# Macaron layer on one core: the second expert list opened with complete sequences 4 and 5, and the last four attention chains moved forward in the slot table

## Chip, core and metric

One NeuronCore of a Trainium2 chip runs the whole kernel. The metric is device time in microseconds (us), the median of several executions. The engines are TensorE (PE, its weight loads PEld), VectorE (DVE), ScalarE (ACT), GpSimd (POOL) and SyncE (SP). Each works through its own instructions in order and waits on semaphores.

## What is computed

Eight sequences of 512 tokens with 128 features (4096 tokens, 32 blocks of 128) go through a sandwich: half an expert layer, a state-space attention layer, half an expert layer.

```
x = x + 0.5 * ffn(layernorm(x))      # 12 experts, top 3 per token
x = x + attn(layernorm(x))           # gates, a scan over time, layernorm, gated projections
x = x + 0.5 * ffn(layernorm(x))      # the same experts again

ffn:  logits = x @ Wg; topw, sel = top_k(logits, 3); w = softmax(topw)
      h = gelu(x @ Wup[e] + bup[e]);  y = h @ Wdown[e] + bdown[e];  out = sum_k w_k y_sel_k
```

## The kernel before

**Tiles and lists.** The expert work is cut into 225 tiles of 128 rows that belong to one expert. For a tile PE does four matmuls up (L1017), ACT four gelus (L1205) and a copy of the expert's weights (L1088), PE four matmuls down (L1032), and DVE adds the bias into `Ys` (L2059). The tiles stand in four lists: list 0 (tiles 0 to 59, first expert layer, sequences 0 to 3), list 1 (tiles 60 to 106, first layer, sequences 4 to 7, with what was left of 0 to 3), list 2 (tiles 107 to 153, second layer, sequences 0 to 2) and list 3 (tiles 154 to 224, second layer, sequences 3 to 7). Within a list the "front" tiles are those that can be filled from the list's first few sequences; `FRONT` (L43) says how many sequences, `GA` (L44) how many groups of four tiles that gives: 3 groups, 12 tiles, for list 1.

**Routing of the rows.** POOL moves rows by indirect DMAs of 128 rows, one for each block of tokens and each of its three choices, so 12 a sequence. A scatter (`scatter_x`, L806) writes a sequence's normalised rows into the list's table `xs`; SP then loads a tile's rows from there (`load_rows`, L646 to L661). Before a list's first load SP waits until the scatters of its `FRONT` sequences have landed. A gather (`gather_y`, L809 to L824) brings a token's three expert rows back from `ys` to `YG`; before the first one of a list it waits until all tiles of the list are stored. In list 3 the expert rows are scattered one transfer a tile (`yk`, L832), with the 36 gathers of list 2 between them. POOL's order is fixed by the table `POOL` (L155): "Y" are the gathers of a sequence after the first expert layer, "K" its scatters for the second.

**Attention chains.** Between the two expert layers each sequence goes through a chain of some 23 steps, which the table `CHAIN` (L130) puts into tile slots of list 1 and 2: the numbers count tiles from tile 60, one column for each sequence. G0 and G2 on DVE add the gathered expert rows to X (L1330), S1 is the norm on DVE (L1279 to L1303), G on ACT writes the normalised rows (L1111), A1 on PE transposes them (L878), A2 to A7 are the projections, T to L choose the experts for the second layer (N on DVE and ACT, L1120), and K counts places so that POOL can scatter (K on PE is L937). Each engine does the steps of a slot after its work on the slot's tile. So a step that is not ready blocks the tiles behind it.

**First lists' tables.** How the tiles of list 0 and list 1 are shared out among experts is worked out on DVE in step Q4 (L1884), at tile 12 of list 0. Tables for list 2 are made by DVE in the steps A0 to A2 at tiles 98 to 100 and Z0 to Y3 at tiles 104 to 111, for list 3 in the same way from tile 147 and tile 159.

**Start of a list.** PE transposes the first four tiles of a new list one by one (`turn_first`, L998): the first of them stands in the last tile of the list before, behind that tile's up matmuls and ahead of the down matmuls of the tile two before it.

Of the kernel before, what the change touches and what calls it, by code (L numbers as in the profile page):

```python
# [10 lines left out]
ALU = mybir.AluOpType  # L11
# [3 lines left out]
P = 128  # L15
# [15 lines left out]
AT = tuple(4 * s[0] for s in SEQS)  # L31
# [337 lines left out]
def macaron_kernel(nc, a, out):  # L369
    with ExitStack() as ctx:  # L370
        def sb(name, shape, dt=F32):
            return ctx.enter_context(nc.sbuf_tensor(name, shape, dt))

        def sem(name):
# [228 lines left out]
        def _(e):  # L603
# [151 lines left out]
        def _(e):  # L755
# [513 lines left out]
        def _(e):  # L1269
# [541 lines left out]
            def second(kind, s):  # L1811
# [57 lines left out]
                elif kind == "Q3":  # L1869
# [14 lines left out]
                elif kind == "Q4":  # L1884
# [31 lines left out]
                    dv.on(e.tensor_tensor(step2[:], basB[:, 0:E], basC[:, 0:E], ALU.subtract))  # L1916
                    e.wait_ge(s_dv, dv.n - 2)
                    dv.on(e.scalar_tensor_tensor(don4[:], rem[:], 0.0, remW[:], ALU.max, ALU.min))
                    e.wait_ge(s_dv, dv.n)
                    dv.on(e.tensor_tensor(don4[:], don4[:], donC[:], ALU.add))  # L1920
                    e.wait_ge(s_dv, dv.n)
# [227 lines left out]
```

## Time and profile before

| | |
|---|---|
| median of 3 runs | 615.02 us (612.63 to 616.59) |
| the profiled execution's own time | 614.01 us |
| its span, first to last instruction | 612.3 us |
| mean granted TensorE clock | 0.973 |
| busy, share of the span | PE 91%, ACT 84%, POOL 66%, DVE 60% |

Busy PE is partly modelled, because matmuls overlap. The times of the rows are us from the start of the span. A share of the span is a mean over stages with different limits, so the stages are read one by one.

### The profile page before, as it was taken

The page shows a single profiled execution, that of the slowest core. Times are in us where ns is not written, and L with a number is a line of the kernel's source. Part 1 is how long each engine was busy: PE and PEld are TensorE (multiplying, and loading weights), DVE is VectorE, ACT ScalarE, POOL GpSimd, SP SyncE. Part 2 cuts the span into 40 slices and gives each one's busy share as a digit, 9 for nine tenths or more (in the row PEclk, how much of TensorE's full clock was granted, in tenths as well). Part 3 has the DMA queues.
Part 4 walks back from the last instruction along what each step waited for, and adds up shares of the span by engine and source line. Part 5 has one row for each costly group of instructions (what it writes and reads, how often), then busy time and mean ns, then how long its engine had stood idle before and what let it go on. Part 6 is the DMA issues. An engine that isn't in the chain of part 4 may idle for free.

```text
span 612.3 us, 17470 instructions
## 1 busy us (share of the span) xinstructions
PE 559.2 (91%) x4625; PEld 523.3 (85%) x4625; DVE 369.6 (60%) x1735; ACT 514.3 (84%) x1462; POOL 403.8 (66%) x424
## 2 busy tenths in 40 slices
PE   6899887999999999989899798998799799999996
PEld 6789887999999888868799697877699799999992
DVE  7977899441111586988775578997727632232225
ACT  4547994799989989889988699988689789989885
POOL 1076577777746777137677777767777777777771
PEclk9789999899999999999999799999999999999999
DMA  7997243243463434112355333232254532433264
GB/s 197 316 234 212 54 135 88 79 131 104 123 180 101 123 87 118 52 48 71 91 160 136 87 88 98 83 107 67 67 148 111 139 89 72 117 90 85 64 232 138
DMA packets 99127, 72.28 MB, mean 118 GB/s; under 512 B 13520, under 2 KB 91910, under 8 KB 99033
## 3 DMA queue, kind: packets, MB, share of 16 engines
q1 hardware_dynamic: 83032, 43.62, 25.7%
q0 software_dynamic: 13024, 26.11, 15.0%
q10 hardware_dynamic: 2976, 1.44, 0.8%
q8 instruction: 42, 0.69, 0.5%
q14 instruction: 53, 0.43, 0.2%
HBM read 37.08 MB, written 34.75 MB: 117 GB/s over the span
## 4 chain that ended last, share of the span: by engine, by line
PE 32%; DVE 21%; POOL 17%; issue 12%; ACT 8%; DMA 7%; ACTq 1%; DVEq 1%; POOLq 0%; SPq 0%
PE ps L1017 12%; PE ps L1032 12%; POOL YG L822 10%; DMA YG<-ys,SY 4%; POOL xs L806 4%; ACT hT L1205 3%; POOL yk L832 3%; DVE YG L1717 2%; DMA yk<-Ys,row 2%; PE ps L1007 2%; DVE st L1274 2%; DVE Ys L2059 1%; DVE X L1330 1%; PE ps L987 1%; DVE X L1316 1%
## 5 line engine op out<-in xcount | busy, mean ns | idle before, releaser
L1205 ACT ACTIVATE hT<-ps,BU 128x128 f32<-128x128 f32 x900 | 261.5, 392 | 43.9 <-PE ps L1017 34.5
L1017 PE MATMUL ps<-xT,WT 128*128 128x128 f32 x1800 | 243.1, 279 | 8.6 <-ACT hT L1205 5.5
L1032 PE MATMUL ps<-WD,hT 128*128 x1800 | 240.9, 277 | 6.8 <-DVE Ys L2059 6.8
L1017 PEld LDWEIGHTS ps<-xT,WT 128*128 128x128 f32 x1800 | 222.9, 194 | 18.2 <-issue 16.4
L1032 PEld LDWEIGHTS ps<-WD,hT 128*128 128x128 f32 x1800 | 221.4, 194 | 8.4 <-issue 8.3
L806 POOL DMA_INDIRECT xs<-XN,SX x144 | 142.4, 989 | 70.7 <-issue 63.3
L822 POOL DMA_INDIRECT YG<-ys,SY x132 | 130.6, 990 | 49.3 <-issue 35.4
L1088 ACT ACTIVATE WT<-WU 128x512 f32 x225 | 150.2, 668 | 7.5 <-DVE eW L1750 3.3
L2059 DVE TENSOR_TENSOR Ys<-ps,BD 128x128 f32<-128x128 f32 x225 | 54.8, 285 | 146.5 <-PE ps L1032 140.4
L832 POOL DMA_INDIRECT yk<-Ys,row x71 | 70.7, 995 | 21.9 <-issue 12.2
L793 POOL DMA_INDIRECT xl<-xna,SG x24 | 23.1, 961 | 37.4 <-DMA xna<-XN 27.6
L1330 DVE SCALAR_TENSOR_TENSOR X<-YG,WK,X 128x128 f32<-128x128 f32 x96 | 26.6, 345 | 13.8 <-DMA YG<-ys,SY 13.2
L1178 ACT ACTIVATE xT<-ps 128x512 f32<-128x512 f32 (+1 forms) x52 | 32.6, 627 | 1.6 <-PE ps L987 0.8
L987 PE MATMUL ps<-ident,xl 128*128 128x128 f32 x205 | 31.3, 275 | 0.0
L1120 ACT ACTIVATE XN<-X,na,nr 128x128 f32<-128x128 f32 x64 | 26.4, 510 | 4.4 <-DVE na L1303 4.4
L793 POOL DMA_INDIRECT xl<-xnc,SG x24 | 23.0, 957 | 7.3 <-issue 5.8
L1316 DVE SCALAR_TENSOR_TENSOR X<-YG,WK,X 128x128 f32<-128x128 f32 x36 | 12.7, 354 | 20.8 <-DMA YG<-ys,SY 19.8
L987 PEld LDWEIGHTS ps<-ident,xl 128*128 128x128 f32 x205 | 24.6, 144 | 0.0
L1007 PE MATMUL ps<-ident 128*128 128x128 f32 x130 | 22.8, 353 | 1.6 <-POOL ident L759 1.6
L1007 PEld LDWEIGHTS ps<-ident 128*128 128x128 f32 x130 | 21.4, 190 | 1.7 <-POOL ident L759 1.6
L1274 DVE BATCH_NORM_STATS2 st<-X 128x6 f32<-128x128 f32 x96 | 21.0, 277 | 0.7 <-DVE SL L1641 0.4
L904 PEld LDWEIGHTS ps<-wgc,sT 128*128 128x128 f32 x128 | 16.0, 197 | 4.5 <-ACT sT L1104 4.0
(366 smaller groups left out, 592.2 us busy)
## 6 DMA issues: line engine op xcount, KB each, us to landing
ys<-Ys SPq DMA_DIRECT2D x41, 256.0 KB
xl<-xs SPq DMA_DIRECT2D x94, 64.0 KB
xl<-xs SPq DMA_DIRECT2D x71, 66.0 KB
WU<-in_L_ffn_Wup_dram SPq DMA_DIRECT2D x12, 256.0 KB, 4.6
WD<-in_L_ffn_Wdown_dram SPq DMA_DIRECT2D x12, 256.0 KB, 4.7
YG<-yk SPq DMA_DIRECT2D x4, 768.0 KB, 6.2
xs<-XN,SX POOLq DMA_INDIRECT x144
YG<-ys,SY POOLq DMA_INDIRECT x132
```

The costliest lines, as they stand in the source:

```text
L793: e.indirect_dma_start(xl[m % NXL][:, k % 4, 0:D], None, xna if k < NA[0] else xnb if k < NM else xnc, bass.IndirectOffsetOnAxis(SG[:, k:k ...
L806: e.indirect_dma_start(xs[n], bass.IndirectOffsetOnAxis(SX[n][:, k, t:t + 1], 0), XN[:, AT[n] + t, 0:DX[n]], None).then_inc(s_air[j % AIR] ...
L822: e.indirect_dma_start(YG[:, (AT[n] + t) % 16, k, :], None, ys[n], bass.IndirectOffsetOnAxis(SY[n][:, t // 4, k, t % 4:t % 4 + 1], 0)).the ...
L832: e.indirect_dma_start(yk, bass.IndirectOffsetOnAxis(row[g % NROW][:, k % 4:k % 4 + 1], 0), Ys[(GROUP0[n] + g) % NYS][:, k % 4, :], None, ...
L987: i = e.transpose(ps[:, j * P:(j + 1) * P], xl[m % NXL][:, j, 0:D], ident[:])
L1007: e.transpose(HB[0][:, 0:P], ident[:], ident[:])
L1017: x = e.matmul(HB[i % 2][:, c * P:(c + 1) * P], WT[i % NW][:, c, :], xT[m % 2][:, j * P:(j + 1) * P], start=True, stop=True)
L1032: x = e.matmul(YB[u % 2][:, j * D:(j + 1) * D], hT[i % 3][:, c * P:(c + 1) * P], WDf[:, bass.ds(r + c * P, P)], start=(c == 0), stop=(c == ...
L1088: e.activation(WT[i % NW][:], WU[:, :, bass.ds(wu_at.pop((GROUP0[n] + k // 4, k % 4)), D)], ACT.Copy).then_inc(s_wt0, 1)
L1205: x = e.activation(hT[i % 3][:, c * P:(c + 1) * P], HB[i % 2][:, c * P:(c + 1) * P], ACT.Gelu, bias=BU[:, bass.ds(b + c, 1)])
L1274: dv.on(e.bn_stats(st6[:, t, :], src))
L2059: e.tensor_tensor(Ys[m % NYS][:, k % 4, :], YB[u % 2][:, j * D:(j + 1) * D], BD[:, bass.ds(bd_at.pop((m, k % 4)), D)], ALU.add).then_inc(s ...
```

## The change

Three things are changed, and the arithmetic of the layer stays the same.

1. `FRONT` of list 1 goes from 3 sequences to 2 and means something else there: the front is now 6 groups, 24 tiles, that hold every row of sequences 4 and 5 (and whatever of 6 and 7 fills those tiles). So their results are complete after tile 83. Step Q4 works this out with six more DVE instructions. SP's wait ahead of a list's first load is now for all the list's scatters, in list 1 and in list 3 too; only list 2 keeps the wait for its front (two sequences).
2. POOL's order gets the gathers of sequences 4 and 5 right behind those of sequence 3, ahead of the scatters of sequences 0 to 2. They wait for the stores of list 1's first 24 tiles alone.
3. In `CHAIN` every step of sequences 4 and 5 moves 8 tiles forward, of sequence 6 some 7, of sequence 7 some 5.

```
-FRONT = (HS, 3, 2, 3)
+FRONT = (HS, 2, 2, 3)

-    ("V", "G0", (8, 13, 19, 27, 54, 58, 65, 72)),
+    ("V", "G0", (8, 13, 19, 27, 46, 50, 58, 67)),
...
-    ("PV", "K", (33, 38, 44, 53, 75, 81, 86, 89)),
+    ("PV", "K", (33, 38, 44, 53, 67, 73, 79, 84)),

-POOL = (("Y", 0), ("Y", 1), ("Y", 2), ("Y", 3), ("K", 0), ("K", 1), ("K", 2), ("Y", 4), ("Y", 5), ("Y", 6), ("Y", 7),
+POOL = (("Y", 0), ("Y", 1), ("Y", 2), ("Y", 3), ("Y", 4), ("Y", 5), ("K", 0), ("K", 1), ("K", 2), ("Y", 6), ("Y", 7),
         ("K", 3), ("K", 4), ("K", 5), ("K", 6), ("K", 7))

                 if g == 0:
-                    for w in scattered(n, FRONT[n]):
+                    for w in scattered(n, FRONT[n] if n == 2 else len(SEQS[n])):
                         e.wait_ge(*w)

-                    for m in range(GROUP0[n + 1] - NYS, GROUP0[n + 1]):
+                if k == 0 and (t == 0 or n == 1 and t == 4 * FRONT[1]):
+                    done = GROUP0[1] + GA[1] if n == 1 and t == 0 else GROUP0[n + 1]
+                    for m in range(done - NYS, done):
```

On POOL, behind the last scatters for list 1, the kernel before has this order (xl are list 0's rows, xs the scatters, YG the gathers, yk the stores of list 3):

```order
L793 DMA xl<-xnc,SG 128x128
L806 DMA xs<-XN,SX 32384x128 x20
L822 DMA YG<-ys,SY 128x128 x48
L806 DMA xs<-XN,SX 32384x128 x36
L822 DMA YG<-ys,SY 128x128 x48
L806 DMA xs<-XN,SX 32384x132 x60
L832 DMA yk<-Ys,row 7680x128 x2
```

and the changed kernel this one:

```order
L794 DMA xl<-xnc,SG 128x128
L807 DMA xs<-XN,SX 32384x128 x20
L826 DMA YG<-ys,SY 128x128 x72
L807 DMA xs<-XN,SX 32384x128 x36
L826 DMA YG<-ys,SY 128x128 x24
L807 DMA xs<-XN,SX 32384x132 x60
L836 DMA yk<-Ys,row 7680x128 x2
```

So 24 gathers now stand ahead of the 36 scatters of sequences 0 to 2, of which the first 24 are those that list 2 waits for.

On DVE, at tiles 106 and 107, the last of list 1 and the first of list 2, the kernel before has A7 of sequence 3 (X<-X,ps) and then tables of list 2:

```order
L2059 TENSOR_TENSOR Ys<-ps,BD 128x128
L1437 TENSOR_TENSOR X<-X,ps 128x512
L1619 TENSOR_TENSOR tk<-tk,stp 1x420
L1622 TENSOR_SCALAR ei<-EF 128x35
L1624 TENSOR_REDUCE RF<-tk 1x35
L2059 ISA
L2059 TENSOR_TENSOR Ys<-ps,BD 128x128
L1629 SCALAR_TENSOR_TENSOR RR<-iotl,RF 1x35
```

and the changed kernel:

```order
L2075 TENSOR_TENSOR Ys<-ps,BD 128x128
L1441 TENSOR_TENSOR X<-X,ps 128x512
L1334 SCALAR_TENSOR_TENSOR X<-YG,WK,X 128x128 x6
L1278 BN_STATS st<-X 128x6 x2
L1623 TENSOR_TENSOR tk<-tk,stp 1x420
L1626 TENSOR_SCALAR ei<-EF 128x35
L1628 TENSOR_REDUCE RF<-tk 1x35
L2075 ISA
L2075 TENSOR_TENSOR Ys<-ps,BD 128x128
L1633 SCALAR_TENSOR_TENSOR RR<-iotl,RF 1x35
```

G0 of sequence 4 has come in between; G2 and S1 of sequence 4 come in the same way at tiles 108 and 109, ahead of the norm N' of sequence 3 at tile 110.

On ACT, behind the gelus of tile 110, the kernel before writes the rows of sequence 3 for the second expert layer (N, L1120):

```order
L1205 ACTIVATE hT<-ps,BU 128x128
L1088 ISA
L1088 ACTIVATE WT<-WU 128x512
L1120 ACTIVATE XN<-X,na,nr 128x128 x4
L1205 ISA
L1205 ACTIVATE hT<-ps,BU 128x128
```

and the changed kernel does so too (L1124), with G of sequence 4 (L1115) behind it:

```order
L1209 ACTIVATE hT<-ps,BU 128x128
L1092 ISA
L1092 ACTIVATE WT<-WU 128x512
L1124 ACTIVATE XN<-X,na,nr 128x128 x4
L1115 ACTIVATE XN<-X,na,nr 128x128 x4
L1209 ISA
L1209 ACTIVATE hT<-ps,BU 128x128
```

G of sequence 4 was behind tile 118 before.

## Rows read from the trace of the kernel before

**Rows 1.** Waits of PE, 195 to 450: total us, times, longest.

```profile
PE ps L878 <- ACT XN L1111: 8.1, 4, 4.7
PE ps L937 <- DVE MC L1377: 4.8, 4, 2.8
```

**Rows 2.** Timeline of PE: start, us, line, out<-in, [idle before <-releaser].

```profile
177.89 0.27 PE L998 MATMUL ps<-ident,xl 128*128 128x128 f32 x1
...
305.45 0.27 PE L998 MATMUL ps<-ident,xl 128*128 128x128 f32 x1
...
319.95 0.60 PE L987 MATMUL ps<-ident,xl 128*128 128x128 f32 x4
...
341.22 1.11 PE L878 MATMUL ps<-ident,XN 128*128 128x128 f32 x4 [4.68 <-ACT XN L1111]
...
442.33 0.20 PE L937 MATMUL ps<-M,LT 128*128 128x48 bf16 x1 [2.83 <-DVE MC L1377]
...
450.40 0.27 PE L998 MATMUL ps<-ident,xl 128*128 128x128 f32 x1
```

**Rows 3.** Busy time by engine (PE, PEld, DVE, ACT, POOL), clock, DMA; one stretch.

```profile
340.00:347.00 7.00, 5.78 (x22) 5.00 (x23) 2.94 (x12) 5.34 (x16) 5.17 (x7) 0.51 0.19 49
```

**Rows 4.** Timeline of SP's queue: start, us, line, loads of list 1, 2, 3.

```profile
171.30 4.36 SPq L661 DMA_DIRECT2D xl<-xs  x8
...
301.25 4.36 SPq L661 DMA_DIRECT2D xl<-xs  x8
...
445.86 4.33 SPq L661 DMA_DIRECT2D xl<-xs  x8
```

**Rows 5.** Timeline of POOL.

```profile
108.41 0.99 POOL L793 DMA_INDIRECT xl<-xnc,SG  x1 [0.30 <-issue]
...
175.86 0.97 POOL L806 DMA_INDIRECT xs<-XN,SX  x1 [0.30 <-issue]
...
268.96 0.99 POOL L806 DMA_INDIRECT xs<-XN,SX  x1 [21.03 <-issue]
...
298.73 0.96 POOL L806 DMA_INDIRECT xs<-XN,SX  x1 [0.30 <-issue]
...
460.53 0.99 POOL L832 DMA_INDIRECT yk<-Ys,row  x1 [0.30 <-issue]
```

**Rows 6.** POOL's groups, 460 to 600: busy, mean ns of one, idle before.

```profile
L832 POOL DMA_INDIRECT yk<-Ys,row x71 | 70.7, 995 | 21.9 <-issue 12.2 <-DMA yk<-Ys,row 4.9 <-DVE Ys L2059 3.6
```

**Rows 7.** Chain that ended last, at 184: start, us, a store's landing.

```profile
183.67 1.69 DMA ys<-Ys
```

**Rows 8.** Busy time by engine as in rows 3, three short stretches of DVE work.

```profile
77.80:80.60 2.80, 2.02 (x16) 1.86 (x16) 2.50 (x21) 2.80 (x9) 2.06 (x3) 1.00 0.17 51
...
335.12:337.22 2.10, 1.42 (x13) 1.18 (x12) 2.10 (x8) 0.09 (x1) 1.49 (x3) 1.00 0.41 112
337.25:339.49 2.24, 0.00 (x0) 0.00 (x0) 1.93 (x14) 0.00 (x0) 1.63 (x3) 1.00 0.15 38
```

**Rows 9.** POOL's groups, 180 to 250, as in rows 6.

```profile
L822 POOL DMA_INDIRECT YG<-ys,SY x48 | 47.4, 987 | 23.7 <-issue 14.3 <-DMA ys<-Ys 9.4
```

**Rows 10.** Timeline of DVE.

```profile
237.83 0.88 DVE L2059 TENSOR_TENSOR Ys<-ps,BD 128x128 f32<-128x128 f32 x4 [0.34 <-PE ps L1032]
...
308.56 0.69 DVE L1437 TENSOR_TENSOR X<-X,ps 128x512 f32<-128x512 f32 x1 [0.24 <-PE ps L977]
...
311.06 0.29 DVE L2059 TENSOR_TENSOR Ys<-ps,BD 128x128 f32<-128x128 f32 x1 [0.71 <-PE ps L1032]
...
312.88 0.29 DVE L2059 TENSOR_TENSOR Ys<-ps,BD 128x128 f32<-128x128 f32 x1 [1.03 <-PE ps L1032]
...
457.59 0.29 DVE L2059 TENSOR_TENSOR Ys<-ps,BD 128x128 f32<-128x128 f32 x1 [1.33 <-PE ps L1032]
```

**Rows 11.** Timeline of ACT.

```profile
319.86 1.65 ACT L1120 ACTIVATE XN<-X,na,nr 128x128 f32<-128x128 f32 x4 [0.96 <-DVE na L1303]
```

**Rows 12.** PE's up matmuls (L1017, eight passes a tile) in one stretch.

```profile
135.00:165.00 30.00, 16.90 (x128) 15.57 (x128) 1.00 0.41 116
```

More of the change, by code:

```diff
@@ L42 @@
 HS = 3
-FRONT = (HS, 3, 2, 3)
-GA = tuple(-((E * (P - 1) - (K * (AT[1] * (n == 1) + 4 * f) - FULL * (n == 1)) * P) // P) // 4 for n, f in enumerate(FRONT))
+FRONT = (HS, 2, 2, 3)
+GA = tuple((K * (AT[1] + 4 * f) + E - FULL) // 4 if n == 1 else -((E * (P - 1) - K * 4 * f * P) // P) // 4
+           for n, f in enumerate(FRONT))
 NA = tuple(4 * g for g in GA)
@@ L428, in macaron_kernel @@
             "wB", "remB", "endB", "basB", "don1", "don2", "donC", "remC", "endC", "basC", "endR", "basR"))
-        donW, remW, endW, basW, don4 = (sb(n, [P, EX]) for n in ("donW", "remW", "endW", "basW", "don4"))
+        donW, remW, endW, basW, don4, remX = (sb(n, [P, EX]) for n in ("donW", "remW", "endW", "basW", "don4", "remX"))
         nt6, remL, endL, basL, dltL, stpL, c6 = donC, remC, endC, basC, basB, step3, mixed
@@ L822, in gather_y @@
                 e.indirect_dma_start(
-                    YG[:, (AT[n] + t) % 16, k, :], None, ys[n],
+                    YG[:, (AT[n] + t) % 16, k, :], None, ys[n][0:(NTL[0] - NM + NA[1]) * P] if n == 1 and t < 4 * FRONT[1] else ys[n],
                     bass.IndirectOffsetOnAxis(SY[n][:, t // 4, k, t % 4:t % 4 + 1], 0)).then_inc(s_air[j % AIR], 16)
@@ L1877, in second @@
                     dv.on(e.tensor_tensor(cnt[:, 0:E], total, c4[:], ALU.add))
-                    dv.on(e.scalar_tensor_tensor(c7[:], part, -float(P - 1), c4[:], ALU.add, ALU.add))
+                    dv.on(e.tensor_tensor(c7[:], part, c4[:], ALU.add))
                     e.tensor_tensor(CT[:, a:], rows, by_token(c4, t), ALU.add).then_inc(s_sl0, 1)
@@ L1901, in second @@
                     dv.on(e.tensor_tensor(remW[:], donW[:], donC[:], ALU.subtract))
-                    e.wait_ge(s_dv, dv.n)
+                    dv.on(e.tensor_tensor(remX[:], nte[:], donW[:], ALU.subtract))
+                    e.wait_ge(s_dv, dv.n - 2)
                     dv.on(e.tensor_tensor_scan(endC[:], one[:], remC[:], float(NM), ALU.mult, ALU.add))
+                    e.wait_ge(s_dv, dv.n - 2)
                     dv.on(e.tensor_tensor_scan(endW[:], one[:], remW[:], 0.0, ALU.mult, ALU.add))
-                    e.wait_ge(s_dv, dv.n)
+                    e.wait_ge(s_dv, dv.n - 2)
+                    dv.on(e.tensor_tensor_scan(rem[:], one[:], remX[:], 0.0, ALU.mult, ALU.add))
+                    e.wait_ge(s_dv, dv.n - 1)
                     dv.on(e.tensor_scalar(endW[:], endW[:], endC[:, E:EX], None, ALU.add))
@@ L1909, in second @@
                     dv.on(e.tensor_scalar(lim3[:], donC[:, 0:E], float(P), None, ALU.mult))
-                    e.wait_ge(s_dv, dv.n - 2)
-                    dv.on(e.tensor_tensor(rem[:], endW[:], remW[:], ALU.subtract))
-                    dv.on(e.tensor_tensor(basW[:], endW[:], donW[:], ALU.subtract))
+                    e.wait_ge(s_dv, dv.n - 4)
+                    dv.on(e.tensor_tensor(rem[:], rem[:], remX[:], ALU.subtract))
+                    e.wait_ge(s_dv, dv.n)
+                    dv.on(e.tensor_scalar(rem[:], rem[:], endW[:, E:EX], None, ALU.add))
                     e.wait_ge(s_dv, dv.n)
                     dv.on(e.tensor_scalar(rem[:], rem[:], -1.0, float(NTL[0] + NA[1]), ALU.mult, ALU.add))
-                    dv.on(e.tensor_tensor(step3[:], basC[:, 0:E], basW[:, 0:E], ALU.subtract))
[L1916 to L1921, printed above, removed]
+                    e.wait_ge(s_dv, dv.n)
+                    dv.on(e.scalar_tensor_tensor(remX[:], rem[:], 0.0, remX[:], ALU.max, ALU.min))
+                    e.wait_ge(s_dv, dv.n)
+                    dv.on(e.tensor_tensor(remW[:], remW[:], remX[:], ALU.add))
+                    dv.on(e.tensor_tensor(don4[:], donW[:], remX[:], ALU.add))
+                    e.wait_ge(s_dv, dv.n - 1)
+                    dv.on(e.tensor_tensor_scan(endW[:], one[:], remW[:], 0.0, ALU.mult, ALU.add))
+                    e.wait_ge(s_dv, dv.n)
+                    dv.on(e.tensor_scalar(endW[:], endW[:], endC[:, E:EX], None, ALU.add))
+                    dv.on(e.tensor_tensor(step2[:], basB[:, 0:E], basC[:, 0:E], ALU.subtract))
+                    e.wait_ge(s_dv, dv.n - 1)
+                    dv.on(e.tensor_tensor(basW[:], endW[:], don4[:], ALU.subtract))
+                    e.wait_ge(s_dv, dv.n)
+                    dv.on(e.tensor_tensor(step3[:], basC[:, 0:E], basW[:, 0:E], ALU.subtract))
                     dv.on(e.tensor_tensor(rem[:], nte[:], don4[:], ALU.subtract))
```

42 rows, old and new, of the table CHAIN are left out of this document.

## Prediction, made before the changed kernel ran

> **What bounds the kernel now.** I read the clock and busy shares first: PE is busy for 91% of the span, so time is to be had only where PE waits, and I went on to PE's waits by releaser, then to PE's timeline around each wait, then back along POOL, SP and DVE. In lists 1 and 2 one group stands out: the transposes that open a chain (A1) wait for the rows that ACT writes in step G, 8.1 us in four waits, one of them 4.7 [rows 1]. That one ends at 341.22 [rows 2]: A1 of sequence 4 at tile 119. It waits because the gathers of sequence 4 stand on POOL behind the scatters of sequences 0 to 2. The wait also costs clock: the granted clock in the seven us from 340 is 0.51, so half rate [rows 3]. Seven us at 0.51 lose 3.4, less the half of the 1.2 us in which PE was idle anyway: 2.8. So what the change goes for is worth 4.7 + 2.8 = 7.5 us.
>
> The reader is to see three more places, where PE does not wait now but is close to it. A list begins with the transpose L998, at 177.89, 305.45 and 450.40 [rows 2], and SP issues the loads it needs at 171.30, 301.25 and 445.86 [rows 4]. For list 2 the load follows the last awaited scatter of POOL (sequence 1's, issued at 298.73 [rows 5]) by 2.5 us: that list starts as soon as POOL lets it, with little to spare. And from 460.53 [rows 5] POOL works without a break to the end: its 71 stores of list 3 have 0.31 us of idle time before them on average [rows 6], the same as transfers that wait for nothing.
>
> **The change part by part.** The sum is made against the profiled execution's 614.0 us, which lies 1.0 below the median of 615.0. "Later" is against the kernel before.
>
> Step 1, list 1's start. SP now waits for all 48 scatters of list 1. The last is issued at 175.86 [rows 5]; with the 2.5 us seen at list 2 the load goes out at 178.4 instead of 171.3. From load to transpose the trace shows 6.6, 4.2 and 4.5 us, none of which is the shortest possible. The nearest thing below is a store that landed 1.7 us after its issue [rows 7]. I take 2.2, near that row, since a landing and one semaphore hop are all that is in it; the bounds are 1.7 and 4.2. So L998 comes at 180.6, 2.7 later (2.2 to 4.7). Behind SP's wait stands the store of tiles 52 to 55, which POOL's first gather awaits; that gather also awaits the store of tile 59, which is later still, so it adds nothing. At lists 2 and 3 it is the same with the stores of tiles 100 to 103 and 147 to 150.
>
> Step 2, six more instructions in Q4. Its later part, 20 instructions and one of the step's neighbour, takes 2.8 us [rows 8], 0.14 each, so 0.8 us, ahead of the one-hot rows that PE waits for in list 0. POOL does not see it: its first transfer with the new indices, at 108.41, waits for nothing [rows 5]. PE comes 0.8 later to list 1 and there waits 0.8 less for step 1. It counts as nothing, and as 0.8 if step 1 were not there.
>
> Step 3, list 2's start. The 48 gathers of 180 to 250 take 47.4 us and, without the first wait, 14.3 between them [rows 9], 1.285 each; 24 more are 30.8. They go into a gap of 21.0 us in which POOL waits for the first scatter of sequence 0 [rows 5]; 0.3 of that is a normal step. So the scatters come 30.8 - 20.7 = 10.1 later than the rest of the kernel. That rest is itself 2.7 later, as the gathers start when list 0 is stored. The spare time at list 2 was 4.2 - 2.2 = 2.0 us. PE waits 10.1 - 2.0 = 8.1 us in tile 106 (7.6 to 10.1), and everything behind it in PE's order, the down matmuls of tiles 104 to 106 included, waits with it. Cover there is none: PE works in order.
>
> Here a rule of the skill bears on the price of a gather. The 48 gathers of rows 9 ran at a mean of 987 ns beside the same DVE steps (G0, G2, S1) as the 24 added ones will. The Trainium skill (SBUF — State Buffer, section "Who interferes with whom") says that GpSimd writes the descriptors of such DMAs through ports that DVE can hold for a whole instruction. By it a gather could take longer the busier DVE is; the trace at hand bears that out only weakly, as the mean shows, and the rival on it stands below.
>
> Step 4, clock. A wait of 4.7 us cost 2.8 us at half rate [rows 3]; one of 8.1 I price the same (0 to 3.4).
>
> Step 5, tiles 106 to 111. When PE goes on, DVE has G0, G2 and S1 of sequence 4 to do between A7 and N' of sequence 3: 2.1 + 2.1 + 2.2 us (G2 and S1 from [rows 8], G0 taken like G2). Of its idle time there, 0.7 and 1.0 us [rows 10] go. So N' ends 4.7 later, and ACT's N, which stood idle 0.96 us for it and then took 1.65 [rows 11], begins 4.7 later. Behind it now comes G of sequence 4, as long again. PE has A1 of sequence 4 behind the transposes of tile 111, which end at 319.95 + 0.60 = 320.5 [rows 2]; in the same frame G ends at 319.86 + 4.7 + 1.65 + 1.6 = 327.8. That is 7.3 us of waiting. Step 4 shortens it: PE itself comes 2.8 later, and DVE's chain, which begins 3.1 us after the restart (308.56 [rows 10] against 305.45), some 1.5, since a tile's down matmuls and A7 ahead of it run at half rate. I take 7.3 - 2.8 + 1.5 = 6.0 (0 to 7.3; nothing, if DVE did more of this ahead than its order shows). In the old order the same G had no neighbour.
>
> Step 6, clock again after that wait: 2.8 (0 to 2.8).
>
> Step 7, what goes. The gathers of sequence 4 begin where the gap of 21.0 us began, at 268.96 - 21.0 + 0.3 + 2.7 = 250.9, and are done 15.4 later; tiles 80 to 83, for whose store they wait, were ready at 238.7 [rows 10], or 241.4 now. G0 asks for them at about 319, so this wait is gone: -7.5 (the 4.7 are sure, the 2.8 of clock nearly so). Sequences 5 to 7 keep their spacing of 4, 8 and 9 tiles (4, 7 and 7 before); I leave the other waits of list 2 as they are, the one of 2.8 at K of sequence 7 [rows 1] included, since its steps T to K still share one slot.
>
> Step 8, list 3's start. SP now waits for the scatters of sequence 7 too. K of sequence 7 ran on PE at 442.33, and from there to L998 it was 8.1 us [rows 2]. Now K is five tiles further ahead, at 128 / 8 = 16 tiles in 30 us [rows 12], 1.88 each: PE needs 17.5 us. POOL's first scatter follows K by 2.9 at most (460.53 less twelve of 1.28 is 445.2); I take 2.2, then 11 x 1.28 to the last issue, 2.5 to the load, 2.2 to the transpose: 21.0. PE waits 3.5 (0 to 6).
>
> Step 9, POOL in list 3. The end is POOL's chain of 71 stores and 36 gathers. It began at 460.53, behind the scatters of sequence 7, though tile 154 had been ready at 457.59 + 0.29 [rows 10]. Those scatters are over before list 3 begins now: -2.6 (0 at the worst).
>
> The sum: 2.7 + 8.1 + 2.8 + 6.0 + 2.8 - 7.5 + 3.5 - 2.6 = 15.8, so 614.0 + 15.8 = 629.8, rounded 630. What is late next is the start of list 2, in place of A1 of sequence 4.
>
> **Rivals.** About 1% is what a measurement of this kernel tells from no change.
>
> A, near even: list 2 starts late, but the chain of sequence 4 comes through at tile 111. For it speaks that DVE stands idle during PE's wait of step 3; against it that A7, G0 and the rest follow, in DVE's order, a store that needs PE. Without steps 5 and 6: 629.8 - 8.8 = 621.0.
>
> B, faster: the 24 gathers fit into POOL's gap, so the scatters are not late and only the old wait goes. That needs 20.7 / 24 = 0.86 us a gather in place of 1.285, or a gap that is longer. Rows 9 speak against it, the gap of 21.0 us speaks for it. Without steps 3 to 6: 614.0 + 2.7 - 7.5 + 3.5 - 2.6 = 610.1, and 606.6 if step 8 is hidden too.
>
> C, slower still: transfers on POOL are drawn out where DVE is busier than now. If each of the 24 gathers and the 24 scatters behind them took 0.2 us more, list 2 would start 48 x 0.2 = 9.6 later: 639.4. The rule named under step 3 would do this. The mean of 987 ns speaks against it.
>
> **How the numbers follow.** The forecast has 0.60, A 0.22, B 0.10, C 0.08. The forecast's own range, its steps at their bounds, is about 614 to 640: below, steps 4, 5 and 8 shrink together; above, 10.1 and 4.7 at the list starts. The range of 611 to 639 takes in A and ends short of B and of C. B counts as faster (0.07) when step 8 hides, else as within 1%, like A: 0.24 for the same, so 0.69 for slower by over 1%.
>
> **What would show it.** Right: PE's transpose L998 at list 2's start has a wait of about 8 us, released by SP's loads, with POOL's gap before the scatters gone; A1 of sequence 4 waits some 6 us for ACT behind tile 111, with a clock near 0.5 after each; no wait of 4 us is left near tile 119; L998 of list 3 waits 2 to 5 us. Wrong: PE passes tile 106 without a wait (then B), or tile 111 (then A), or POOL's transfers there show a mean well over 1.0 us (then C).

## Result, and the profile after the change

The changed kernel takes 648.09 us (median of 4 runs, 645.83 to 649.98) against 613.83 us for the kernel before on the same chip (611.92 to 616.59): a ratio of 1.055, 95% interval 1.049 to 1.061. Slower was right; the size was not: the change costs 34 us, where the prediction had 15.8 and a range that ended at 639. The profiled execution took 649.49.

From the profile's page: the span, PE's busy time, and the granted clock in 40 slices.

```profile
span 647.8 us, 17478 instructions
PE 575.5 (89%) x4625; PEld 537.7 (83%) x4625; DVE 371.6 (57%) x1741; ACT 516.7 (80%) x1462; POOL 405.1 (63%) x424
PEclk8788997999999999999787999899799999999999
```

The waits of PE in lists 1 and 2 of the changed kernel (195 to 485 us; total, times, longest), to be held against [rows 1]:

```profile
PE ps L882 <- ACT XN L1115: 11.2, 4, 6.4
PE ps L1002 <- DMA xl<-xs: 8.2, 2, 5.1
PE ps L941 <- DVE MC L1381: 7.6, 3, 4.2
PE ps L882 <- DVE X L1441: 2.6, 1, 2.6
PE ps L978 <- DVE tg L1437: 1.8, 1, 1.8
```

The same waits in PE's timeline (start, us, line, out<-in, idle before and releaser), the start of list 1 (184.52) included:

```profile
184.52 0.30 PE L1002 MATMUL ps<-ident,xl 128*128 128x128 f32 x1 [2.29 <-DMA xl<-xs]
320.26 0.45 PE L1002 MATMUL ps<-ident,xl 128*128 128x128 f32 x1 [5.11 <-DMA xl<-xs]
345.12 1.12 PE L882 MATMUL ps<-ident,XN 128*128 128x128 f32 x4 [6.36 <-ACT XN L1115]
386.05 1.12 PE L882 MATMUL ps<-ident,X 128*128 128x128 f32 x4 [2.59 <-DVE X L1441]
405.38 0.39 PE L978 MATMUL ps<-BO,ones 3*128 3x512 bf16 x1 [1.78 <-DVE tg L1437]
419.02 0.20 PE L941 MATMUL ps<-M,LT 128*128 128x48 bf16 x1 [2.96 <-DVE MC L1381]
463.90 0.22 PE L941 MATMUL ps<-M,LT 128*128 128x48 bf16 x1 [4.19 <-DVE MC L1381]
484.53 0.44 PE L1002 MATMUL ps<-ident,xl 128*128 128x128 f32 x1 [3.11 <-DMA xl<-xs]
```

In the order of the rows: the starts of lists 1 and 2; A1 of sequence 4 at tile 111; T of sequence 4 at tile 125; A7 of sequence 5 at tile 130; K of sequence 5; K of sequence 7; the start of list 3. The first three and the last were forecast. The four between them were not: there the kernel before has one wait above 1.3 us, the one of 2.83 at K of sequence 7 [rows 2].

Busy time by engine (PE, PEld, DVE, ACT, POOL), granted clock, DMA share and GB/s in eight stretches of the changed kernel. The last is the whole of list 2, from its first transpose to that of list 3:

```profile
317.30:327.50 10.20, 7.07 (x29) 6.15 (x30) 2.62 (x9) 2.57 (x9) 7.76 (x9) 0.50 0.52 155
341.20:348.00 6.80, 2.88 (x14) 2.89 (x15) 6.02 (x34) 5.68 (x15) 5.28 (x6) 0.50 0.20 54
385.60:389.00 3.40, 2.95 (x14) 2.95 (x15) 3.04 (x18) 3.08 (x9) 0.00 (x0) 0.50 0.51 140
406.00:409.40 3.40, 3.40 (x18) 3.40 (x17) 3.14 (x13) 0.00 (x0) 2.49 (x4) 0.51 0.49 143
419.70:423.10 3.40, 3.40 (x18) 3.40 (x17) 2.16 (x14) 2.67 (x7) 0.16 (x1) 0.50 0.00 0
460.70:467.50 6.80, 3.60 (x19) 3.60 (x20) 5.31 (x34) 2.94 (x9) 1.71 (x3) 0.50 0.05 16
484.50:487.90 3.40, 3.19 (x14) 2.94 (x15) 0.29 (x1) 1.84 (x6) 0.00 (x0) 0.51 0.50 120
...
320.26:484.53 164.27, 138.53 (x999) 125.49 (x1000) 107.66 (x510) 121.75 (x335) 93.41 (x94) 0.89 0.28 82
```

and the whole of list 2 in the kernel before:

```profile
305.45:450.40 144.95, 130.01 (x1001) 117.64 (x1000) 109.23 (x513) 122.89 (x339) 107.79 (x111) 0.96 0.36 100
```

So list 2 grew by 19.3 us with the same work: PE is idle 25.7 us of it in place of 14.9, and busy 8.5 longer, at a mean clock of 0.89 in place of 0.96. The half clock that was forecast is there around the two long waits (317.3 and 341.2), and it is there with the shorter ones too (385.6, 406.0, 419.7, 460.7).

A ledger from the three list starts (177.89, 305.45, 450.40 before [rows 2]; 184.52, 320.26, 484.53 after) and the two spans:

| part | measured | forecast |
|---|---|---|
| until list 1 starts | +6.6 | +2.7 (step 1) |
| list 1, until list 2 starts | +8.2 | +8.1 (step 3) |
| list 2, until list 3 starts | +19.3 | +7.6 (steps 4 to 8) |
| list 3 and the end | +1.4 | -2.6 (step 9) |
| sum | +35.5 | +15.8 |

Of the 19.7 us that the forecast lacks, 3.9 lie ahead of list 1, 11.7 in list 2 and 4.0 in list 3.

### The profile page after: what moved, and what is told of

The parts are those of the page before. It is cut to its first block and busy times, and to the rows that moved or that the text cites. A ratio compares the mean times of both kernels' runs of the same rounds, so it can differ in the third digit from the quotient of the medians.

```text
span 647.8 us, 17478 instructions
## 1 busy us (share of the span) xinstructions
PE 575.5 (89%) x4625; PEld 537.7 (83%) x4625; DVE 371.6 (57%) x1741; ACT 516.7 (80%) x1462; POOL 405.1 (63%) x424
## 5 line engine op out<-in xcount | busy, mean ns | idle before, releaser
L1021 PE MATMUL ps<-xT,WT 128*128 128x128 f32 x1800 | 250.1, 284 | 8.8 <-ACT hT L1209 5.7
L1036 PE MATMUL ps<-WD,hT 128*128 x1800 | 245.4, 281 | 6.4 <-DVE Ys L2075 5.5
L1021 PEld LDWEIGHTS ps<-xT,WT 128*128 128x128 f32 x1800 | 229.3, 199 | 18.0 <-issue 15.8
L1036 PEld LDWEIGHTS ps<-WD,hT 128*128 128x128 f32 x1800 | 226.1, 197 | 8.1 <-issue 8.1
L807 POOL DMA_INDIRECT xs<-XN,SX x144 | 144.0, 1000 | 81.1 <-issue 59.0
L826 POOL DMA_INDIRECT YG<-ys,SY x132 | 130.2, 986 | 55.6 <-issue 35.7
L836 POOL DMA_INDIRECT yk<-Ys,row x71 | 70.7, 996 | 36.3 <-DVE Ys L2075 18.4
L1124 ACT ACTIVATE XN<-X,na,nr 128x128 f32<-128x128 f32 x64 | 26.4, 508 | 8.8 <-DVE na L1307 8.8
L1199 ACT ACTIVATE xT<-ps 128x128 f32<-128x128 f32 x20 | 5.5, 275 | 23.9 <-PE ps L1002 23.9
L882 PE MATMUL ps<-ident,XN 128*128 128x128 f32 x64 | 11.3, 308 | 12.1 <-ACT XN L1115 11.2
```

What stands on the lines that cost most here:

```text
L807: e.indirect_dma_start(xs[n], bass.IndirectOffsetOnAxis(SX[n][:, k, t:t + 1], 0), XN[:, AT[n] + t, 0:DX[n]], None).then_inc(s_air[j % AIR] ...
L826: e.indirect_dma_start(YG[:, (AT[n] + t) % 16, k, :], None, ys[n][0:(NTL[0] - NM + NA[1]) * P] if n == 1 and t < 4 * FRONT[1] else ys[n], ...
L836: e.indirect_dma_start(yk, bass.IndirectOffsetOnAxis(row[g % NROW][:, k % 4:k % 4 + 1], 0), Ys[(GROUP0[n] + g) % NYS][:, k % 4, :], None, ...
L1021: x = e.matmul(HB[i % 2][:, c * P:(c + 1) * P], WT[i % NW][:, c, :], xT[m % 2][:, j * P:(j + 1) * P], start=True, stop=True)
L1036: x = e.matmul(YB[u % 2][:, j * D:(j + 1) * D], hT[i % 3][:, c * P:(c + 1) * P], WDf[:, bass.ds(r + c * P, P)], start=(c == 0), stop=(c == ...
```

## Experiments

Thirteen more kernels ran. The theories when they began: T1, POOL's order costs most (list 2 is late); T2, the slot table does (chain steps collide on DVE); T3, SP's longer waits do. One table serves all: the median and the 95% interval of its ratio to the kernel before, which ran beside each group of them (medians 613.1 to 613.9); from one profiled execution each, the first transpose of list 1 (L998 of before, L1001 or L1002), the lengths of list 1 and list 2 from first transpose to first transpose, and the rest of the span.

| kernel | us | ratio | list 1 starts | list 1 | list 2 | rest |
|---|---|---|---|---|---|---|
| before | 613.8 | | 177.9 | 127.6 | 145.0 | 161.9 |
| changed | 648.1 | 1.049 to 1.061 | 184.5 | 135.7 | 164.3 | 163.3 |
| e1 old slots | 638.6 | 1.038 to 1.050 | 179.7 | 137.5 | 154.4 | 164.3 |
| e2 old slots and POOL | 634.1 | 1.030 to 1.038 | 181.4 | 129.2 | 156.8 | 164.3 |
| e3 sequence 5's gathers later | 640.3 | 1.038 to 1.046 | 182.6 | 130.2 | 163.3 | 162.5 |
| e4 old 6, 7 | 650.2 | 1.056 to 1.063 | 181.7 | 138.2 | 164.1 | 164.2 |
| e5 all by 8 | 620.5 | 1.008 to 1.014 | 180.0 | 130.2 | 146.0 | 160.7 |
| e6 all by 5 | 627.8 | 1.020 to 1.027 | 181.1 | 130.0 | 151.3 | 161.4 |
| e7 4, 5 by 5 | 633.0 | 1.028 to 1.035 | 181.6 | 129.3 | 157.8 | 160.6 |
| e8 6 by 8 | 630.0 | 1.020 to 1.033 | 180.1 | 130.0 | 154.9 | 164.3 |
| e9 old slots, old list 3 wait | 622.8 | 1.013 to 1.019 | 181.1 | 130.6 | 147.2 | 161.9 |
| e10 as e5, G of 4 early | 620.3 | 1.009 to 1.017 | 180.1 | 131.8 | 145.6 | 161.3 |
| e11 split only | 618.6 | 1.007 to 1.015 | 181.6 | 128.7 | 144.6 | 161.1 |
| e12 sequence 4's gathers only | 613.7 | 0.999 to 1.003 | 182.5 | 129.5 | 139.1 | 160.6 |
| e13 as e5, G of 4 earlier still | 623.5 | 1.014 to 1.019 | 181.2 | 137.3 | 143.0 | 160.3 |

### First: slots, POOL's order, SP's waits

**e1**, the slot table of before in the changed kernel (all rows of CHAIN, two shown):

```
-    ("V", "G0", (8, 13, 19, 27, 46, 50, 58, 67)),
+    ("V", "G0", (8, 13, 19, 27, 54, 58, 65, 72)),
...
-    ("PV", "K", (33, 38, 44, 53, 67, 73, 79, 84)),
+    ("PV", "K", (33, 38, 44, 53, 75, 81, 86, 89)),
```

> The changed kernel with the slot table CHAIN of the kernel before; POOL's new order, the new split of list 1 and the longer waits of SP stay. Theory T1 (POOL's order is what costs most: the 24 gathers delay the scatters and list 2 starts some 9 us late, and no chain step lies in a bad place): about 630 to 635, L1002 at list 2 waits 5 us or more, A1 of sequence 4 at tile 119 waits under 1 us. Theory T2 (most of the loss is the slot table: chain steps collide on DVE in tiles 106 to 153 and PE waits at A1, T, A7 and K): about 620 to 625, the short waits of tiles 124 to 153 gone. If neither, about 648 as the changed kernel.

**e2**, POOL's order of before on top of that:

```
+POOL = (("Y", 0), ("Y", 1), ("Y", 2), ("Y", 3), ("K", 0), ("K", 1), ("K", 2), ("Y", 4), ("Y", 5), ("Y", 6), ("Y", 7),
```

> The changed kernel with CHAIN and POOL of the kernel before; what is left of the change is the new split of list 1 (six instructions more in Q4) and SP's waits for all scatters of lists 1 and 3. T1 and T2 alike: 614 + 2.7 for list 1's start, less than 1 for Q4, and nothing to 4 at list 3's start, so 617 to 621. T3 (the longer waits of SP carry a large part of the loss): 625 or more, with a wait of 3 us or more in L1002 at list 1 and at list 3 and later A1 waits in list 1.

**e3**, the changed kernel with another order on POOL:

```
+POOL = (("Y", 0), ("Y", 1), ("Y", 2), ("Y", 3), ("Y", 4), ("K", 0), ("K", 1), ("Y", 5), ("K", 2), ("Y", 6), ("Y", 7), ("K", 3), ("K", 4), ("K", 5), ("K", 6), ("K", 7))
```

> The changed kernel with the 12 gathers of sequence 5 moved on POOL behind the scatters of sequences 0 and 1 (order Y0 to Y4, K0, K1, Y5, K2, Y6, Y7, K3 to K7). Twelve gathers of 1.285 are 15.4 us and fit into the gap of 21 us. T1: list 2 starts on time, L1002 there waits under 1 us, 9 us less, and the half clock behind it goes too: 636 to 639. T2: list 2 starts on time, but PE then meets the chain of sequence 4 earlier, and the wait at tile 111 grows by as much as was won: 645 or more.

**e4**, the columns of sequences 6 and 7 alone as before:

```
-    ("V", "G0", (8, 13, 19, 27, 46, 50, 58, 67)),
+    ("V", "G0", (8, 13, 19, 27, 46, 50, 65, 72)),
```

> The changed kernel with the columns of sequences 6 and 7 in CHAIN as in the kernel before (7 and 5 tiles later); sequences 4 and 5 stay 8 tiles forward. T2, if the crowding of four chains in fewer tiles is what costs in tiles 124 to 153: the waits at T of sequence 4, A7 and K of sequence 5 and K of sequence 7 shrink, 636 to 641. If each chain meets the same DVE work wherever it stands: within 3 of the changed kernel's 648. List 2's late start and the wait at tile 111 stay in either case.

Measured 638.6, 634.1, 640.3 and 650.2. No theory holds alone: 638.6 fits none of the three, 640.3 lies between what T1 and T2 gave, 634.1 is in the range of T3, with the waits that T3 named, and 650.2 came where each chain was to meet the same work wherever it stands, but for another reason. T1 is right for its part: with POOL's order eased (e3), list 1 is 5.6 us shorter than in the changed kernel, and e1 against e2 says the same from the other side (137.5 and 129.2). What I had left out is the same in e1, e2 and e4: with the old column, K of sequence 7 stands five tiles before list 3, and SP now waits for its scatters. The wait at list 3 is 13.2 us in e1 and 13.3 in e4; PE's timeline of e2:

```profile
467.42 0.45 PE L1002 MATMUL ps<-ident,xl 128*128 128x128 f32 x1 [13.77 <-DMA xl<-xs]
```

So the wait for all scatters and the earlier column of sequence 7 belong together. In e4 the waits at T of sequence 4 and A7 of sequence 5 were gone (T2), but a wait of 13.28 at list 3 hid it in the sum.

### Second: the distance between the chains

In the table of before, S1 of sequence 6 stands at slot 69 and S3 of sequence 5 at 70; in the changed one both stand at slot 62, since chains 4 and 5 moved by 8 and chain 6 by 7. Theory R says that these changed distances cost the time, theory D that any chain costs it that moves into the full tiles 107 to 140. e5 to e8 stand on e3 and change CHAIN alone (row G0 shown; each column moves as a whole):

```
-    ("V", "G0", (8, 13, 19, 27, 46, 50, 58, 67)),
+    ("V", "G0", (8, 13, 19, 27, 46, 50, 57, 64)),
+    ("V", "G0", (8, 13, 19, 27, 49, 53, 60, 67)),
+    ("V", "G0", (8, 13, 19, 27, 49, 53, 58, 67)),
+    ("V", "G0", (8, 13, 19, 27, 46, 50, 57, 67)),
```

(the four + rows are e5, e6, e7, e8 in this order).

> As e3 (12 gathers of sequence 5 behind the scatters), and in CHAIN all four chains of sequences 4 to 7 exactly 8 tiles forward of the kernel before, so that they stand to each other as they did there. Theory R (the waits of tiles 124 to 150 come from chains 6 and 7 having moved by 7 and 5 where 4 and 5 moved by 8, so that norms of one chain now stand on DVE just ahead of steps that PE waits for): they go back to those of the kernel before, 8 to 12 less in tiles 124 to 150, and list 3 starts without a wait of SP's loads since K of sequence 7 is 8 tiles ahead (3 less): 625 to 631 against 640 in e3. Theory D (density: any chain moved into tiles 107 to 140 meets the table steps of list 2 and the gathers of sequences 6 and 7, which end at 369): 637 or more, with DVE waiting for YG at G0 or G2 of sequence 7. The wait at tile 111 stays in both.

> As e3, and all four chains 5 tiles forward of the kernel before. K of sequence 7 stands where it is in the changed kernel, so list 3 starts as there. G of sequence 4 then comes 3 tiles behind N of sequence 3. My step 5 (the wait at tile 111 is DVE's G0, G2 and S1 of sequence 4 ahead of N' of sequence 3, and ACT's G behind its N): the wait of 6 us and its half clock go, 8 less. Theory R adds 8 to 12 less in tiles 124 to 150: 620 to 626 against 640 in e3. Theory D: only the 8 or less, 632 to 638.

> As e3, with sequences 4 and 5 5 tiles forward in place of 8; sequences 6 and 7 as in the changed kernel (7 and 5). Step 5 alone: the wait at tile 111 goes, 8 less, so about 632. Whether the waits of tiles 124 to 150 stay tells whether they hang on chains 6 and 7 (R and D: chains 4 and 5 now stand 2 tiles later against 6 than in the kernel before, so new neighbours; waits of some size stay, 628 to 636).

> As e3, with sequence 6 8 tiles forward in place of 7, so that chains 4, 5 and 6 stand to each other as in the kernel before; sequence 7 stays 5 forward. R: the waits at T of sequence 4 and at A7 of sequence 5 (tiles 125 and 130, 2.9 and 1.8 us in e3, each with 3.4 us at half clock behind) go, those at K of sequences 5 and 7 stay: 632 to 636. D: within 2 of e3's 640.

Measured 620.5, 627.8, 633.0 and 630.0 against 640.3 in e3: e5 and e8 lie 4.5 and 2.0 us below what R gave, e6 between the ranges of R and D, e7 within its range. The clearest is e8: one column, by one tile, and 10.3 us less, 8.4 of them in list 2. DVE's timeline of the changed kernel ahead of PE's wait at 386.05 (start, us, line, operation):

```profile
378.78 0.87 DVE L1278 BATCH_NORM_STATS2 st<-ps 128x6 f32<-128x128 f32 x4
...
381.79 0.16 DVE L1307 SCALAR_TENSOR_TENSOR na<-mv,nr 128x4 f32<-128x4 f32 x1
381.87 0.37 DVE L1283 BATCH_NORM_AGGREGATE mv<-st 128x2 f32<-128x6 f32 x4
...
383.95 0.16 DVE L1307 SCALAR_TENSOR_TENSOR na<-mv,nr 128x4 f32<-128x4 f32 x1
384.52 0.89 DVE L2075 TENSOR_TENSOR Ys<-ps,BD 128x128 f32<-128x128 f32 x4 [0.41 <-issue]
385.32 0.68 DVE L1441 TENSOR_TENSOR X<-X,ps 128x512 f32<-128x512 f32 x1
```

The norm S3 of sequence 5 (from PSUM, 378.78) and the norm S1 of sequence 6 (381.87) stand back to back, 5.3 us, ahead of four bias adds and the A7 add of sequence 4, for which T waits on PE. In e8 the norm of sequence 6 ended before S3 began; DVE's and PE's timelines there:

```profile
367.85 0.16 DVE L1306 SCALAR_TENSOR_TENSOR na<-mv,nr 128x4 f32<-128x4 f32 x1
367.93 0.88 DVE L1277 BATCH_NORM_STATS2 st<-ps 128x6 f32<-128x128 f32 x4
...
372.35 0.68 DVE L1440 TENSOR_TENSOR X<-X,ps 128x512 f32<-128x512 f32 x1
```

```profile
373.08 0.66 PE L881 MATMUL ps<-ident,X 128*128 128x128 f32 x4 [0.32 <-DVE X L1440]
```

The wait at T is 0.32, the one at A7 of sequence 5 is gone from the list of waits, and so is the half clock behind them. With all four chains by 8 (e5) the distances of before are back throughout, K of sequence 7 stands 8 tiles ahead, and list 2 is as long as before (146.0 and 145.0). So theory R holds for the waits at T of sequence 4 and A7 of sequence 5. It does not hold for K of sequence 7. e6, which keeps the distances too but moves by 5, is 7 us slower than e5, with a wait of 2.00 at list 3 and this one:

```profile
441.64 0.22 PE L940 MATMUL ps<-M,LT 128*128 128x48 bf16 x1 [4.16 <-DVE MC L1380]
```

That wait is 4.1 to 4.2 us wherever this K stands at tile 144 (the changed kernel, e3, e6, e7, e8), 2.40 at tile 141 (e5) and 2.7 to 2.8 at tile 149 (before, e1, e2, e4), so it goes by the place and not by the distance. In e6 the bias adds of a tile stand on DVE between the add of A7 and the norm of sequence 7 (433.23 and 436.18), in e5 the norm follows at once (425.36 and 426.08). So the step from e8 to e5, three tiles for sequence 7, is not distance alone.

My own step 5 is borne out in part only. In e6 and e7, G of sequence 4 is no longer behind N of sequence 3, yet A1 waits 5.2 and 3.6 us three tiles later. The wait moved with the chain.

### Third: single parts alone

**e9** has the old CHAIN, POOL's order of e3, and the old wait ahead of list 3; **e11** the same with POOL's old order; **e12** the same with this order:

```
-                    for w in scattered(n, FRONT[n] if n == 2 else len(SEQS[n])):
+                    for w in scattered(n, FRONT[n] if n >= 2 else len(SEQS[n])):
...
+POOL = (("Y", 0), ("Y", 1), ("Y", 2), ("Y", 3), ("Y", 4), ("K", 0), ("K", 1), ("K", 2), ("Y", 5), ("Y", 6), ("Y", 7), ("K", 3), ("K", 4), ("K", 5), ("K", 6), ("K", 7))
```

**e10** and **e13** are e5 with the first four steps of sequence 4 ahead (two of the four rows; the + rows are e10, then e13, whose G2 and S1 stand at 42 and 43, and at 36 and 37):

```
-    ("V", "G0", (8, 13, 19, 27, 46, 50, 57, 64)),
+    ("V", "G0", (8, 13, 19, 27, 40, 50, 57, 64)),
+    ("V", "G0", (8, 13, 19, 27, 35, 50, 57, 64)),
...
-    ("A", "G", (13, 19, 26, 32, 50, 56, 63, 70)),
+    ("A", "G", (13, 19, 26, 32, 44, 56, 63, 70)),
+    ("A", "G", (13, 19, 26, 32, 38, 56, 63, 70)),
```

> The changed kernel with the old CHAIN, POOL's order of e3 (only sequence 4's gathers ahead of the scatters) and SP's wait ahead of list 3 for its first three sequences alone, as in the kernel before. What is left of the change: the split of list 1 with SP's wait there, and the gathers of sequence 4 ahead. By my steps 1, 2 and 7, with the sizes measured since (list 1's start 4 to 5, the wait at tile 119 and its clock 5 to 7.5 less): 611 to 614, so within 1% of the kernel before. If the early gathers cost something I don't see, 616 or more.

> As e5 (620), with G0, G2, S1 (DVE) and G (ACT) of sequence 4 six tiles further ahead still, at tiles 100 to 104; its A1 and what follows stay where they are. The gathers of sequence 4 are done at about 268, long before tile 100. Step 5 (the wait of 6.0 us at tile 111 is DVE's norm S1 of sequence 4 with N' of sequence 3, and ACT's G behind its N): the wait goes, with most of its 6.8 us at half clock, 610 to 613. Rival (DVE is full there with the tables of list 2 and N' of sequence 3 is late anyway, or the moved steps make PE wait at tiles 100 to 106): 616 to 620.

> As e2 (634), with SP's wait ahead of list 3 for its first three sequences alone, as in the kernel before; CHAIN and POOL of the kernel before. So only the split of list 1, Q4 and SP's wait at list 1 are left. If e2's 13.8 us wait at list 3 and its half clock are step 8 as it works with the old slots: 16 less, 617 to 619. If the split does harm elsewhere: 622 or more.

> As e9, with sequence 5's gathers behind all three scatters of list 2 (order Y0 to Y4, K0, K1, K2, Y5, Y6, Y7, K3 to K7), so that only sequence 4's gathers have moved; old CHAIN, list 3's wait as in the kernel before. If e9's 7.5 us wait in tile 118 (loads of list 2 that need the scatters of sequence 2) came from the 12 gathers of sequence 5 ahead of these: it goes, and with the wait at tile 119 gone too (step 7) and list 1 starting 4 to 5 later, 611 to 615. If step 7's gain does not show even so: 618 or more.

> As e10, with G0, G2, S1 and G of sequence 4 at tiles 95 to 98 in place of 100 to 104, ahead of the tables A0 to A2 of list 2. If the waits of PE at tiles 104 to 107 in e10 (1.7 and 3.6 us) came from DVE being full at tiles 98 to 106 only: they go and the one at tile 111 stays away, 610 to 614. If DVE is full in the whole stretch from tile 92 to 112: the wait comes up once more in another place, 617 to 621.

Measured 622.8, 620.3, 618.6, 613.7 and 623.5.

e11 came as expected: without the longer wait at list 3 it is 15.5 us below e2, and the split of list 1 with SP's wait there costs 5 us (1.007 to 1.015). That is what is left of T3.

e9 missed, by a wait I had not seen. PE's timeline, and POOL's last gather of sequence 5 with the first scatter of sequence 2 behind it:

```profile
342.12 1.09 PE L990 MATMUL ps<-ident,xl 128*128 128x128 f32 x4 [7.52 <-DMA xl<-xs]
```

```profile
320.01 1.13 POOL L825 DMA_INDIRECT YG<-ys,SY  x1 [0.30 <-issue]
321.44 1.00 POOL L806 DMA_INDIRECT xs<-XN,SX  x1 [0.30 <-issue]
```

The tiles of list 2 behind its front need the scatters of sequence 2, and these stood behind twelve gathers. e12 takes those away, and PE's waits in lists 1 and 2 there are

```profile
PE ps L881 <- ACT XN L1114: 4.9, 4, 1.5
PE ps L940 <- DVE MC L1380: 4.7, 4, 2.7
```

that is, the wait of 4.7 at A1 of sequence 4 [rows 1] is gone and nothing has come in its place: list 2 takes 139.1 in place of 144.6 in e11. That is the whole gain of the early gathers, 5 us, and the split that they need costs as much: 613.7 against 613.1 for the kernel before in the same batch, ratio 0.999 to 1.003. No version tried beats the kernel before.

e10 and e13 removed the wait at tile 111 and kept the time, or lost 3 us, so they came out as their rivals had it, e13 2.5 us above even that range. PE's timeline of e10 at tiles 104 to 106 (K of sequence 2, A7 of sequence 3), then of e13 (K of sequence 1 at tile 98, and loads of list 2):

```profile
306.40 0.20 PE L940 MATMUL ps<-M,LT 128*128 128x48 bf16 x1 [1.70 <-DVE MC L1380]
...
317.26 0.60 PE L977 MATMUL ps<-BO,ones 3*128 3x512 bf16 x1 [3.64 <-DVE tg L1436]
```

```profile
292.02 0.22 PE L940 MATMUL ps<-M,LT 128*128 128x48 bf16 x1 [4.64 <-DVE MC L1380]
...
348.00 0.88 PE L990 MATMUL ps<-ident,xl 128*128 128x128 f32 x3 [3.93 <-DMA xl<-xs]
```

Three of these four waits are on DVE. The likely reason stands in the kernel before: busy times (the third is DVE) in three stretches of 20 us around list 2's start.

```profile
270.00:290.00 20.00, 19.35 (x148) 16.76 (x148) 17.20 (x82) 17.69 (x47) 15.05 (x16) 1.00 0.23 72
290.00:310.00 20.00, 17.60 (x139) 15.62 (x139) 16.42 (x82) 18.01 (x48) 13.43 (x15) 1.00 0.37 110
310.00:330.00 20.00, 19.67 (x176) 19.39 (x175) 14.68 (x77) 18.33 (x58) 15.43 (x16) 1.00 0.52 146
```

DVE is 73 to 86% busy there, where its share of the whole span is 60%, and the 6.4 us of G0, G2 and S1 find no free place in it. The old slots, tiles 114 to 117, lie at its end and behind it. The fourth wait, 3.93 us in e13, is another: SP's load goes out at 343.52, 2.6 behind POOL's last scatter of sequence 2, which stands behind the gathers of sequence 5 as in e9. Neither e10 nor e13 ran with POOL's order of e12, so what early steps of sequence 4 are worth with it is open.

## Why the prediction was right in direction and wrong in size

**Step 1** holds as a mechanism: SP's load goes out at 182.57, 2.5 behind POOL's last scatter at 180.03, and PE waits 2.29. The start is 6.6 later, not 2.7, as that scatter itself is 4.2 late. POOL is late by as much long before, at its first transfer with the new indices:

```profile
112.36 0.99 POOL L794 DMA_INDIRECT xl<-xnc,SG  x1 [0.30 <-issue]
```

That is 4.0 behind the kernel before (108.41 [rows 5]). The thirteen experiments, which have the same instructions up to there, are at 107.6 to 110.3 and start list 1 1.8 to 4.7 later. So the 3.9 us beyond the forecast do not come from step 1's wait; equal code shows a spread of nearly 3 us there, and the cause of the rest is open. **Step 2** can't be told apart in these runs.

**Steps 3 and 4** were right in the path: no gap ahead of the scatters is left on POOL (0.30 us before the first), list 1 is 8.2 longer (8.1), and from 317.3, within the wait, there are 10.2 us at half clock, in which PE is busy 7.07: 3.5 lost (2.8). The wait itself is 5.11, below the 7.6 to 10.1 that step 3 gave: POOL's chain sets when list 2 starts, and PE was itself later by the other 3.1 us. In list 1 it is busy 1.0 longer and its A1s wait 4.8 us in place of 3.4, at a granted clock of 1.00 until 317.3. Where list 2's loads are on time (e2, e3, e5 to e9, e11, e12), list 1 is still 1.1 to 3.0 us longer than before, by 1.1 and 1.6 with POOL's old order (e11, e2).

```profile
285.03 1.12 POOL L826 DMA_INDIRECT YG<-ys,SY  x1 [0.30 <-issue]
286.46 1.00 POOL L807 DMA_INDIRECT xs<-XN,SX  x1 [0.30 <-issue]
```

**Steps 5 and 6**: 6.36 us at tile 111 (6.0), by the path that the prediction named; ACT's timeline, N of sequence 3, then G of sequence 4, then PE at 345.12:

```profile
341.88 1.65 ACT L1124 ACTIVATE XN<-X,na,nr 128x128 f32<-128x128 f32 x4 [4.89 <-DVE na L1307]
343.43 1.63 ACT L1115 ACTIVATE XN<-X,na,nr 128x128 f32<-128x128 f32 x4
```

Its clock cost some 1.4: 3.4 of the 6.8 us, less half of the 3.9 in which PE was idle (2.8). That it was the order of N and G, as step 5 has it, is only the near cause; in e6, e7, e10 and e13 the wait moved with the steps, which fits a DVE that is full there.

**Step 7**: the old wait went, as forecast; alone it is worth 5 us (e11 to e12), not 7.5; 1.22 of waiting stays at that A1. **Step 8**: 3.11 us (3.5), by the path named: from K of sequence 7 to list 3's first transpose it is 20.6 us (21.0).

**The step that failed** is the sentence at the end of step 7. It saw that the spacing of the chains changes ("4, 8 and 9 tiles (4, 7 and 7 before)") and went on: "I leave the other waits of list 2 as they are". List 2 is 19.3 - 7.6 = 11.7 us longer than forecast. Of that 6.0 is idle time of PE: it grew by 10.8 (25.7 less 14.9), of which the steps that came account for 6.4 - 4.7 + 3.1 = 4.8; of the other 6.0, the groups of K, T and A7 hold 5.3 (7.2, 2.6 and 1.8 us in list 2, against 4.4, 0.7 and 1.2). The other 5.7 is busy time, which I read as clock: PE is busy 8.5 longer, where steps 4, 6 and 7 had 2.8 + 2.8 - 2.8. Moving one chain by one tile takes back 10.3 us of the median and 8.4 of list 2 (e3 to e8). K of sequence 7, which the same sentence kept at 2.8 because its steps share one slot as before, waits 4.19; that goes by its place, as e6 shows.

**Step 9** had the wrong sign. POOL's scatters were over in time, as forecast, but its first store of list 3 then waits for DVE's bias add, which waits for PE:

```profile
494.22 1.00 POOL L836 DMA_INDIRECT yk<-Ys,row  x1 [13.19 <-DVE Ys L2075]
...
L836 POOL DMA_INDIRECT yk<-Ys,row x71 | 70.7, 996 | 36.3 <-DVE Ys L2075 18.4 <-issue 12.5 <-DMA yk<-Ys,row 4.6
```

The step took tile 154 to be ready 7.5 us behind the list's first transpose, as before. It was 9.4 (the add ends at 493.94), for the most part since PE begins the list at half clock: 3.4 us at 0.51 from 484.5, in which it is busy 3.19. So the first store comes 9.7 us behind that transpose (10.1 before), and 0.4 of the 2.6 came in. From the first store to the end it is 153.6 us, against 151.8. The second row is POOL's group of stores in list 3: 18.4 us of its idle time hang on DVE's adds, 13.2 of them ahead of the first store and 5.2 behind it, where it was 3.6 [rows 6].

**The rivals.** A (no stall at tile 111) and B (24 gathers fit into the gap) did not come. C, longer transfers on POOL beside a busy DVE, did not either: the 72 gathers of the changed kernel run at a mean of 967 ns, the 48 of before at 987 [rows 9], and the 24 scatters behind them at 971 (983 before). The Trainium skill's rule on shared ports (SBUF — State Buffer, section "Who interferes with whom") shows no effect here.

```profile
L826 POOL DMA_INDIRECT YG<-ys,SY x72 | 69.6, 967 | 35.5 <-issue 21.6 <-DMA ys<-Ys 13.9
```

## What to carry to other kernels

Where several chains of steps run interleaved on in-order engines, their distances from one another are part of the tuning: with all four moved by 8 (e5) the kernel is 7 us above the one before, 5 of which the split of list 1 costs alone (e11); moving them by 8, 8, 7 and 5 (e3) costs some 20 more, part of it by the place of sequence 7. Equal distances are not enough: all by 5 (e6) is 7 us above all by 8. So price a table of slots by asking, for each engine, which steps now share a slot or stand ahead of one that another engine waits for. And before moving work forward into a stretch, read the busy share of each engine in that stretch, not over the span: where DVE was 73 to 86% busy, the steps that e10 and e13 brought in were followed by a wait in a new place.

## What was not expected of the hardware

How cheaply the clock is lost. A wait of PE of 1.78 us (405.38) and one of 2.59 (386.05) were each followed by 3.4 us at a granted clock of 0.50 or 0.51, the lower of the two levels, 1.2 GHz. Behind the first PE was busy for all of these 3.4 us (406.00 in the stretches above), so 1.7 us were lost, as much as the wait itself. It isn't a rule one can plan by: in e8 a wait of 2.37 us, at K of sequence 5, cost no clock, as the stretch behind it shows.

```profile
400.00:403.40 3.40, 3.05 (x18) 2.09 (x19) 2.99 (x22) 2.57 (x7) 0.68 (x1) 1.00 0.18 58
```

The Trainium skill (TensorE: Matmul & The Clock Gate, section "HAM oscillation — how this bites in real kernels") tells of a kernel in which a wait on DMAs between groups of matmuls throws the clock back each time. The short stretches at 0.50 above agree that such waits cost clock again and again, but here they are waits on DVE and ACT as well as on DMAs, and not each of them did.
